# Attention and top-2 experts on one core: the product with the values in 64-row halves

## The reference

```python
x = L0_attn_x                                  # (8, 512, 128)
h = layernorm(x)
Q, K, V = (h @ W.T + b for each)               # 16 heads of 8
attn = softmax(Q @ K.T / sqrt(8), axis=-1)
x = x + (attn @ V) @ Wo.T + bo
h = layernorm(x)
logits = h @ Wr.T + br                         # 8 experts
top_v, top_i = top_k(logits, 2); top_w = softmax(top_v)
tgt2 = sum over the chosen e of top_w * (relu(h @ W1[e].T + b1[e]) @ W2[e].T + b2[e])
x = x + layernorm(h + tgt2) * gamma + beta
```

## Time and profile before

| what | value |
|---|---|
| median of 3 runs | 753.96 us (751.37 to 755.16) |
| the profiled execution | 752.29 us, its span 750.5 us |
| beats 0 to 127, first to last score pair A | 33.8 to 493.6 us |
| experts' stage | about 560 to 750.5 us |
| busy: TensorE, VectorE, ScalarE | 609.3, 489.0, 447.4 us |
| TensorE clock granted, mean | 0.91 |

### The profile page before, as it was taken

The page is one execution under the profiler, slowest core; times in us unless marked ns, Lnnn a source line. Parts: engine busy times, 40 slices in busy tenths (PEclk is TensorE's granted clock), DMA queues, the critical chain, the costliest instruction groups (busy, mean ns, idle before and its releaser), DMA issues. The chain is left out here.

```text
span 750.5 us, 13269 instructions
## 1 busy us (share of the span) xinstructions
PE 609.3 (81%) x3750; PEld 321.2 (43%) x3750; DVE 489.0 (65%) x1319; ACT 447.4 (60%) x945; POOL 242.6 (32%) x454
## 2 busy tenths in 40 slices
PE   2899999879988997987987998995229998999680
PEld 1633333323333432332332333332128988888530
DVE  3579989968967985985995887751204444444357
ACT  2718888867956965875885786683114444544333
POOL 5200101150240332214115005016425665555534
PEclk9959999989998998998998899899559999999976
DMA  7552122122122122022112211000121221221193
GB/s 219 195 153 66 44 69 83 49 67 74 37 85 72 33 84 84 26 65 89 49 47 70 65 45 48 6 0 30 50 83 54 65 66 56 69 66 57 47 238 98
DMA packets 54216, 54.47 MB, mean 73 GB/s; under 512 B 8286, under 2 KB 37514, under 8 KB 54164
## 3 DMA queue, kind: packets, MB, share of 16 engines
q1 hardware_dynamic: 48372, 44.19, 20.8%
q0 software_dynamic: 4416, 8.53, 3.2%
q10 hardware_dynamic: 1376, 1.13, 0.5%
HBM read 29.01 MB, written 24.81 MB: 72 GB/s over the span
## 5 line engine op out<-in xcount | busy, mean ns | idle before, releaser
L643 DVE TENSOR_REDUCE mneg<-s_psum 128x1 f32<-128x512 f32 x512 | 325.9, 684 | 89.5 <-PE s_psum L810 55.7
L546 ACT ACTIVATE pt<-st_psum 128x512 f32<-128x512 f32 x512 | 279.9, 598 | 93.3 <-PE st_psum L826 82.7
L826 PE MATMUL st_psum<-qs,ks 64*128 64x512 f32 x512 | 202.5, 471 | 24.8 <-ACT pt L546 19.4
L810 PE MATMUL s_psum<-ks,qs 64*128 64x512 f32 x512 | 208.3, 482 | 3.3 <-DVE mneg L643 2.1
L896 PE MATMUL pv_psum<-pt,vst 128*16 128x512 f32 x1024 | 142.8, 632 | 0.0
L810 PEld LDWEIGHTS s_psum<-ks,qs 64*128 64x128 f32 x512 | 84.4, 196 | 120.2 <-DVE mneg L643 94.9
L826 PEld LDWEIGHTS st_psum<-qs,ks 64*128 64x128 f32 x512 | 82.4, 193 | 69.1 <-ACT pt L546 52.7
L1099 ACT ACTIVATE hid<-h_psum,b1c 128x256 f32<-128x256 f32 x144 | 57.2, 474 | 71.2 <-PE h_psum L1204 69.3
L1062 POOL DMA_INDIRECT results<-res,goal_now x72 | 71.6, 994 | 33.7 <-issue 33.7
L1211 PE MATMUL y_psum<-w2t,hid 128*128 128x128 f32 x576 | 73.1, 280 | 0.0
L1211 PEld LDWEIGHTS y_psum<-w2t,hid 128*128 128x128 f32 x576 | 68.9, 194 | 0.9 <-issue 0.2
(11 more groups left out here) (164 smaller groups left out, 711.3 us busy)
## 6 DMA issues: line engine op xcount, KB each, us to landing
parts<-high SPq DMA_DIRECT2D x32, 256.0 KB, 3.0
ks<-parts SPq DMA_DIRECT2D x128, 48.0 KB
qs<-parts SPq DMA_DIRECT2D x128, 48.0 KB
lot<-sent SPq DMA_DIRECT2D x37, 132.0 KB
parts<-low SPq DMA_DIRECT2D x16, 256.0 KB, 3.1
got<-results SPq DMA_DIRECT2D x16, 256.0 KB, 5.1
xres<-in_L_attn_x_dram SPq DMA_DIRECT2D x8, 256.0 KB, 3.6
pt<-in_L_ffn_W_dram SPq DMA_DIRECT2D x1, 2048.0 KB, 14.5
```

The lines of the kernel that those rows point to most:

```text
L546: nc.scalar.activation(pt[:, n % PT_SLOTS, (g + 2) % 4, :], st_psum[:, k % ST_BANKS, :], ACT.Exp, scale=SCALE).then_inc(exp_done, 1)
L643: nc.vector.tensor_reduce(mneg[:, (n // 4) % 2, at:at + 1], s_psum[:, k % S_BANKS, :], AX_X, ALU.max, negate=True).then_inc(max_done, 1)
L810: mm(s_psum[:, k % S_BANKS, :], qs[rows, c, P * (n % 4):P * (n % 4) + P], ks[rows, c, g, :], start=True, stop=True).then_inc(s_made, 1)
L826: mm(st_psum[:, k % ST_BANKS, :], ks[rows, c, g, P * (n % 4):P * (n % 4) + P], qs[rows, c, :], start=True, stop=True).then_inc(st_made, 1)
```

## The change

The values product is split: each head's 128 rows become two halves of 64 rows, and each half has a bank of its own (`pv_psum` has 2 banks, and `st_psum` 2 instead of 3). The weights are windows of 32 columns in a new layout of `vst`, so that an even quad lands in rows 0 to 15 of each 32 and the odd quad after it in rows 16 to 31; one accumulation holds two quads, over 8 units. The heads of a quad are dealt out accordingly (`head_of`). The copy to `pvs` takes both banks once in 8 beats. TURN comes once in 8 beats (17 + 8m); for each of 4 pieces two matmuls with the identity add the halves. K moves from beat -13 to -11, so from 3 to 5 of 16. The transposes of W2 move from the beats -4 to -1 to the beats 1 to 4.

```diff
--- before.py
+++ after.py
@@ -56,7 +56,7 @@
 LAST_BEAT = GROUPS * (B - 1) + 38
 PLACE_STEPS = 1 + TILES + 5
 S_BANKS = 3
-ST_BANKS = 3
+ST_BANKS = 2
 PT_SLOTS = 4
 COMPLETE_LAG = 3
 KQ_LOADS = 2 * 4 + 1
@@ -75,13 +75,24 @@
     return q if r == 0 and 0 <= q < QUADS * B else None
 
 
+def per_pair(T, offset):
+
+    m, r = divmod(T - offset, 8)
+    return m if r == 0 and 0 <= m < QUADS * B // 2 else None
+
+
+def head_of(c, g):
+
+    return 8 * (c // 2) + 2 * g + c % 2
+
+
 def early_tasks(T):
 
     if (q := per_quad(T, 4)) is not None:
         yield "SHIFT", q
-    if (q := per_quad(T, 13)) is not None:
-        yield "TURN", q
-    for kind, offset in (("XT", -14), ("K", -13), ("Q", -10), ("V", 7), ("OT", 26), ("O", 27), ("X2T", 30),
+    if (m := per_pair(T, 17)) is not None:
+        yield "TURN", m
+    for kind, offset in (("XT", -14), ("K", -11), ("Q", -10), ("V", 7), ("OT", 26), ("O", 27), ("X2T", 30),
                          ("LOGITS", 31)):
         if (b := once(T, offset)) is not None:
             yield kind, b
@@ -118,7 +129,9 @@
 
 def expert_weights(T):
 
-    return range(2 * (T + 8), 2 * (T + 8) + 2) if -8 <= T < 0 else ()
+    if -8 <= T < -4:
+        return range(2 * (T + 8), 2 * (T + 8) + 2)
+    return range(E + 2 * (T - 1), E + 2 * (T - 1) + 2) if 1 <= T < 5 else ()
 
 
 def tiles(b, j=0, count=TILES):
@@ -180,11 +193,11 @@
 
         qs = sb("qs", [P, QUADS, S], F32R)
         ks = sb("ks", [P, QUADS, 4, S], F32R)
-        vst = sb("vst", [P, 2, TILES, H, 16])
+        vst = sb("vst", [P, 2, TILES, H // 2, 64])
         pt = sb("pt", [P, PT_SLOTS, 4, S])
-        pvs = sb("pvs", [P, S])
+        pvs = sb("pvs", [P, 2, S])
         onorm = sb("onorm", [P, TILES, D])
-        rden = sb("rden", [P, TILES, 4])
+        rden = sb("rden", [P, TILES, 8])
         mneg = sb("mneg", [P, 2, TILES * 4])
         shift_rows = sb("shift_rows", [TILES * 4, 2, P], F32R)
         xt, ot, xt2 = sb("xt", [P, 2, S]), sb("ot", [P, S]), sb("xt2", [P, S])
@@ -250,7 +263,7 @@
 
         s_psum = psum("s_psum", S_BANKS)
         st_psum = psum("st_psum", ST_BANKS)
-        pv_psum = psum("pv_psum")
+        pv_psum = psum("pv_psum", 2)
         side_psum = psum("side_psum")
 
         w_loaded, b_loaded, x0_loaded, x1_loaded, x_loaded = (
@@ -336,7 +349,7 @@
                 for g in range(4):
                     rows = slice(32 * g, 32 * g + 3 * HD)
                     dst = ks[rows, c, g] if w == 0 else qs[rows, c]
-                    sp.dma_start(dst.bitcast(F32), parts[b % 2, w, 4 * c + g]).then_inc(kq_in[c], 16)
+                    sp.dma_start(dst.bitcast(F32), parts[b % 2, w, head_of(c, g)]).then_inc(kq_in[c], 16)
 
             def beat(T):
                 if (q := per_quad(T, 4)) is not None:
@@ -345,7 +358,7 @@
                         sp.wait_ge(shift_in, 16 * q)
                     sp.dma_start(qs[SHIFT_ROW:P:32, q % QUADS].bitcast(F32), shift_rows[:, q % 2, :].bitcast(F32))\
                         .then_inc(shift_in, 16)
-                if (b := once(T, -13)) is not None:
+                if (b := once(T, -11)) is not None:
                     store_parts(0, b)
                 if (b := once(T, -10 if T < 0 else -8)) is not None:
                     store_parts(1, b)
@@ -397,7 +410,7 @@
             first_norm(0)
             nc.gpsimd.memset(vst[:], 0.0).then_inc(pool_consts, 1)
             pool.wait_ge(pool_consts, 4)
-            nc.gpsimd.memset(vst[:, :, :, :, HD:HD + 1], 1.0).then_inc(pool_consts, 1)
+            nc.gpsimd.memset(vst[:].rearrange("p z j h (a r) -> p (z j h a) r", r=32)[:, :, HD:HD + 1], 1.0).then_inc(pool_consts, 1)
             nc.gpsimd.memset(tail[:], 0.0).then_inc(tail_ready, 1)
             pool.wait_ge(tail_ready, 1)
             nc.gpsimd.memset(tail[:, :, D].bitcast(U32), NOWHERE).then_inc(tail_ready, 1)
@@ -522,8 +535,8 @@
                         act.wait_ge(pool_consts, 5)
                     if of >= 2:
                         act.wait_ge(pv_made, GROUPS * (of - 1))
-                    nc.scalar.copy(vst[:, of % 2, :, :, 0:HD],
-                                   side_psum[:, 0, :].rearrange("p (j h d) -> p j h d", j=TILES, d=HD))\
+                    nc.scalar.copy(vst[:, of % 2].rearrange("p j h (a r) -> p (j h a) r", r=32)[:, :, 0:HD],
+                                   side_psum[:, 0, :].rearrange("p (x d) -> p x d", d=HD))\
                         .then_inc(side_done, 1)
                 else:
                     dst = {"XT": xt[:, of % 2], "OT": ot[:], "X2T": xt2[:]}[kind]
@@ -531,11 +544,11 @@
 
             def beat(T):
 
-                if (q := per_quad(T, 12)) is not None:
-                    act.wait_ge(pv_made, 4 * q + 4)
-                    if q >= 1:
-                        act.wait_ge(side_made, SIDE["TURN", q - 1] + 1)
-                    nc.scalar.copy(pvs[:], pv_psum[:, 0, :]).then_inc(pv_copied, 1)
+                if (m := per_pair(T, 16)) is not None:
+                    act.wait_ge(pv_made, 8 * m + 8)
+                    if m >= 1:
+                        act.wait_ge(side_made, SIDE["TURN", m - 1] + 1)
+                    nc.scalar.copy(pvs[:], pv_psum[:]).then_inc(pv_copied, 1)
                 n = st_of(T)
                 for g in range(4):
                     if n is not None:
@@ -651,14 +664,14 @@
                                                    in1=high[:, w, :].bitcast(F32), op0=ALU.add, op1=ALU.subtract)\
                         .then_inc(side_done, 1)
                 elif kind == "TURN":
-                    c = of % QUADS
+                    at = 8 * (of % 2)
                     dve.wait_ge(side_made, SIDE["TURN", of] + 1)
-                    sums = side_psum[:, 0, :].rearrange("p (j g r) -> p j g r", j=TILES, g=4)
+                    sums = side_psum[:, 0, :].rearrange("p (j h r) -> p j h r", j=TILES, h=8)
                     nc.vector.reciprocal(rden[:], sums[:, :, :, HD]).then_inc(rden_done, 1)
                     dve.wait_ge(rden_done, of + 1)
                     nc.vector.tensor_tensor(
-                        onorm[:].rearrange("p j (h d) -> p j h d", d=HD)[:, :, 4 * c:4 * c + 4, :],
-                        sums[:, :, :, 0:HD], rden[:].unsqueeze(3).to_broadcast([P, TILES, 4, HD]),
+                        onorm[:].rearrange("p j (h d) -> p j h d", d=HD)[:, :, at:at + 8, :],
+                        sums[:, :, :, 0:HD], rden[:].unsqueeze(3).to_broadcast([P, TILES, 8, HD]),
                         ALU.mult).then_inc(side_done, 1)
                 elif kind == "O":
                     dve.wait_ge(side_made, SIDE["O", of] + 1)
@@ -849,7 +862,8 @@
                 elif kind == "TURN":
                     pe.wait_ge(pv_copied, of + 1)
                     for j in range(TILES):
-                        ins = nc.tensor.transpose(bank[:, P * j:P * j + P], pvs[:, P * j:P * j + P], ident[:])
+                        mm(bank[:, P * j:P * j + P], pvs[:, 0, P * j:P * j + P], ident[:], start=True, stop=False)
+                        ins = mm(bank[:, P * j:P * j + P], pvs[:, 1, P * j:P * j + P], ident[:], start=False, stop=True)
                 elif kind == "XT":
                     pe.wait_ge(xn_done, of + 1)
                     for j in range(TILES):
@@ -888,13 +902,17 @@
                 pe.wait_ge(exp_done, 4 * n + 4)
                 if n % GROUPS == 0:
                     pe.wait_ge(side_done, SIDE["V", b] + 1)
-                if n % 4 == 0 and q > 0:
-                    pe.wait_ge(pv_copied, q)
+                if n % 8 == 0 and n > 0:
+                    pe.wait_ge(pv_copied, n // 8)
                 if n == 0:
                     pe.wait_ge(pv_blank, 1)
                 for g in range(4):
-                    ins = mm(pv_psum[32 * g:32 * g + 16, 0, :], vst[:, b % 2, n % 4, 4 * (q % QUADS) + g, :],
-                             pt[:, n % PT_SLOTS, g, :], start=(n % 4 == 0), stop=(n % 4 == 3))
+                    at = 16 * (q % 2)
+                    for half in range(2):
+                        rows = slice(64 * half, 64 * half + 64)
+                        ins = mm(pv_psum[32 * g:32 * g + 32, half, :],
+                                 vst[rows, b % 2, n % 4, 4 * (q % QUADS // 2) + g, at:at + 32],
+                                 pt[rows, n % PT_SLOTS, g, :], start=(n % 8 == 0), stop=(n % 8 == 7))
                 ins.then_inc(pv_made, 1)
 
             def beat(T):
```

## The result

The change makes the kernel slower: 819.18 us, the median of four runs (815.68 to 819.90), against 752.78 us (751.37 to 755.16) for the kernel before. The ratio is 1.0881 with an interval of 1.0847 to 1.0915. The forecast was 770 us with a range up to 786: the direction is right, the size is not. The profiled execution took 819.55 us, its span is 817.7 us.

The account below looks back on a forecast made before the run. No engine is full in beats 0 to 127; the order of work inside a beat bounds the kernel. 5 + 10 + 14 - 2 + 4 - 11 - 1 = +19 us on 752.3 gave 771, forecast 770; range 735 to 786, from the bounds 757 to 788.

Parts of the forecast that it names:

- the stall: Unexplained standstill of 4.55 us in beat 56, alike in beats 40 to 120 by 16; could move a few us either way.
- Part 1: PV in 64-row halves: sixteen records beside each other, change of form still paid, 0.04 us a beat, +5 us.
- the first rival: Around PV: no change of form between 64-row products, saving 31 us, 740 us; sign PV to A under 0.9 us; chance 0.34.
- rival of halves in turn: PV's halves don't run beside each other, 0.85 us more in 122 beats, +104, 875 us; chance 0.04.
- Part 2: Two banks for turned scores: C and D wait for their own beat's exponentials, 1.3 us a round, +10 us, at most 37.
- the floor: Shortest beat with two banks, the next A at 3.05 us; side tasks of 0.9 us or more hide it.
- Part 3: TURN for two quads: sixteen records, 1.95 us, in beats 1 and 9, +14 us; VectorE's fewer operations -2 us.
- Part 4: Copy to `pvs` of 1024 columns takes 1.06 us, delaying exponentials in beats 0 and 8: +4 us.
- Part 5: K from beat 3 to 5, away from COUNTS: 2.1 us in each of 5 rounds, -11 us.
- Part 6: W2's transposes in beats 1 to 4: scores some 3 us earlier, 2 us taken back in the beats, -1 us.
- The parts cancel: Whole kernel: slack hides two banks' and the copy's costs, TURN costs 12 us; put at 752 us; chance 0.10.

Follow-up runs that it names:

- e9: The changed kernel unedited, on a chip without the stall: 761.98 us against 712.19 for the kernel before, 1.0698.
- e1: The kernel before with two banks instead of three for the turned scores, nothing else changed: 740.79 against 712.69 us, 1.0406.
- e13: The changed kernel with TURN transposing the first half's sums alone, the second half's copied but left out: 794.40 against 748.11 us, 1.0643.
- e3: The kernel before with two quads per PV bank over all 128 rows, three banks, TURN once in 8 beats: 710.16 us, 0.9970.
- e14: As e13, and the copy to `pvs` takes the first half's bank alone: 788.21 against 748.11 us, 1.0565.
- e4: As e3, with K in beat 5 instead of 3: 706.70 us, 0.9906 of the kernel before.
- e12: e4's kernel with an edit to spread GpSimd's indirect DMAs that did not take effect, in effect a repeat: 703.29 against 712.19 us, 0.9865.
- e2: The kernel before with W2's transposes moved to beats 1 to 4, nothing else changed: 716.42 against 712.69 us, 1.0052.
- e15: The changed kernel with one head of four in PV, weights of 32 columns, no reciprocal; one run on a chip with the stall: 790.23 us.
- e16: As e15, with PV's weights 128 columns wide, the score matmuls' own form; one run: 775.58 us.
- e7: As e3, with two banks for the turned scores: 780.72 us, 1.0415 of the kernel before.
- e10: The kernel before with an ineffective edit to spread indirect DMAs, in effect a repeat without the stall: 712.34 against 712.19 us, 0.9998.
- e5: The changed kernel unaltered, again on a chip with the stall: 813.38 against 748.48 us, 1.0895.
- e18: e4's kernel again, on a chip with the stall: 751.34 us, 0.9972 of the kernel before.
- e11: The changed kernel with an ineffective edit to spread indirect DMAs, in effect a repeat without the stall: 761.44 against 712.19 us, 1.0695.
- e8: The changed kernel with W2's transposes back in beats -4 to -1: 814.07 us, 1.0901 of the kernel before.
- e6: The kernel before unaltered, one run on a chip with the stall: 748.94 us.

## Why the prediction was off

Undisturbed by the stall the change costs 49.8 us (e9), where +19 was forecast. The parts measured one by one sum to 54.7; most were measured once, in one surrounding kernel, and each is uncertain by some us:

| part | forecast | measured | from |
|---|---|---|---|
| 1 PV in halves | +5 | +4 | a spacing, 0.03 to 0.04 us a beat; isolated by no run |
| 2 two banks | +10 | **+28** | e1; some 23 of it within the change |
| 3 TURN | +14 | +19 | e13 |
| 3 two quads, fewer operations | -2 | -2.5 | e3 |
| 4 copy | +4 | +6 | e14 |
| 5 K | -11 | -3.5 or -7.5 | e4 less e3, e12 less e3 |
| 6 W2 | -1 | +3.7 | e2 |
| stall | "a few us" | +17 | 66.4 less 49.8 |

The sum uses -3.5 for K. The 5 us that it has too many are within the scatter, but a cause of that size can be named: in e1 the scores begin 6.5 us late because the transposes of W1 and W2 both go through two banks. In the change W2's stand elsewhere, and the scores begin at 31.5 against 29.6 in e2 with three banks, 1.9 us late. So 4.6 of e1's 28 us are not in the change. The rows of parts 3 and 4 compare only in sum: the forecast counts each from the kernel before, e13 and e14 from a kernel with TURN and copy once in 8 beats, which e3 brings in. Together they were forecast at +16 and measured 22.5.

Two steps of the arithmetic were wrong by themselves. The sum of +19 belongs on the median of 753.96, which gives 773, not 770. And the range up to 788 "from the bounds" leaves room for +36 us, while the upper bounds of the parts add up to +96 (27 + 37 + 29 - 2 + 7 - 6 + 4); the +49.8 without the stall lies within those.

**Part 1 was right.** The change of form is not free, so the first rival (740 us) is refuted by its own criterion: PV to A is 1.02 us, not under 0.9, and e15 against e16 shows why. The cost of a change was taken as 0.09 and 0.20; it measured about 0.1 and 0.22. What the rival promised was too much, besides: taking 0.32 us out of each of 122 beats, 39 us, gave 14.7 in two single runs (e15 less e16), with the stall's 3.9 in it. Where the rest went is not shown. The eight tiles run beside each other: PV's sixteen records take 1.09 us against 1.05 for eight of 128 rows, which refutes the rival of halves in turn. In the beats without a side task of round 0 (9 to 11) a beat takes 3.15 to 3.16 us in e9 and 3.12 in e1, and PV to the next A is 1.02 us in place of 0.98, in the medians; 0.01 of that is there in e7 too, with windows of 32 columns over all rows. So the halves add about 0.03 to 0.04, 4 us.

**Part 2 is the step that failed most**: +28 us by itself and some 23 within the change, forecast +10. "D follows at about 1.75 ... the next A at 3.05" was right to 0.1 us. Median lengths of a beat, by its place in the round of 16, of e10 (before), e1 (two banks alone) and e9 (the whole change), none with the stall:

| beat of 16 | 0 | 1 | 2 | 3 | 4 | 5 | 8 | 9 | 10 | 12 | 13 | 14 |
|---|---|---|---|---|---|---|---|---|---|---|---|---|
| e10 | 2.76 | 3.51 | 3.01 | 4.85 | 4.66 | 2.90 | 2.69 | 2.90 | 2.98 | 3.26 | 2.89 | 3.84 |
| e1 | 3.18 | 3.81 | 3.14 | 4.88 | 3.27 | 3.12 | 3.18 | 3.11 | 3.12 | 3.18 | 3.11 | 3.71 |
| e9 | 3.68 | 4.33 | 3.61 | 3.73 | 3.30 | 3.40 | 3.73 | 4.33 | 3.22 | 3.26 | 3.15 | 3.68 |

With two banks no beat of these is under 3.11 us: the floor is there, as forecast, in the beats that were below it. A whole round grows by 1.96 us (from the means over seven rounds), against the forecast's 1.3. That mixes in the clock's dips in beat 4, five in e10 and two in e1: a round with K and without a dip takes 55.8 us in e1 and 53.2 in e2, 2.5 us more, so this half of the step was low by nearly a factor of two. Beats 0 and 8, where the copy holds the exponentials back, and beat 1 grew by 0.3 to 0.5 us, and so did beats 11 and 15 by 0.2 and 0.4, whose long tasks I had called cover. The larger half of the miss is the count: "some 122 beats that have scores and PV, 7.6 rounds" takes a bank's loss to be one of the steady beat. Beats 16 to 127 hold 13.3 of the 26.5 us between the two spans. The start holds 6.5 (the weights' transposes go through the same banks; I wrote +1 for it, under part 6, and within the change it is 1.9), beats 8 to 16 2.7, and the beats behind the last score pairs 5.7, for which I counted nothing. The upper bound of 37 us held.

**Part 3** had TURN's length right, and its place in the long beat. The block in beat 65, TensorE:

```profile
288.22 0.39 PE L823 MATMUL s_psum<-ks,qs 64*128 64x512 f32 x1
...
288.55 0.49 PE L865 MATMUL side_psum<-ident,pvs 128*128 128x128 f32 x2
...
290.21 0.39 PE L866 MATMUL side_psum<-ident,pvs 128*128 128x128 f32 x2
290.53 0.49 PE L839 MATMUL st_psum<-qs,ks 64*128 64x512 f32 x1
```

288.55 to 290.53 is 1.98 us, forecast 1.95. Beats 1 and 9 grew by 0.52 and 1.22 us from e1 to e9, forecast 0.86 and 1.2. Undoing it (e5 to e13) takes 0.52 and 1.18 us out of these two and 0.24 and 0.06 out of beats 2 and 10 behind them: 2.0 us a round, against the forecast's 2.06. The steady rounds were right, then; the rest of the 19 us lies in the stalled beat 8 and behind beat 127, and partly in the scatter of the medians. **Part 4**: the copy takes 1.01 us (forecast 1.06) and costs 6 us, not 4: the added 0.42 us comes through almost in full, 15 times.

**Part 5** was the "sure gain" of 11 us. The beats came out as forecast. The beats that answer to the earlier trace rows, the starts of A in beats 99, 100 and 101:

```profile
427.65 0.49 PE L823 MATMUL s_psum<-ks,qs 64*128 64x512 f32 x1
...
431.38 0.49 PE L823 MATMUL s_psum<-ks,qs 64*128 64x512 f32 x1
...
434.68 0.49 PE L823 MATMUL s_psum<-ks,qs 64*128 64x512 f32 x1
```

They take 7.03 us in place of 9.35, forecast about 7. But the reason was only half seen. Beats 100 and 116 of the kernel before, behind K with COUNTS and behind COUNTS alone (columns: stretch, its us, busy us of TensorE, its loads, VectorE, ScalarE and GpSimd, then TensorE's granted clock, DMA share and GB/s):

```profile
391.83:396.33 4.50, 3.82 (x18) 0.93 (x18) 2.71 (x5) 2.31 (x5) 2.26 (x10) 0.70 0.56 177
452.36:455.62 3.26, 2.58 (x18) 0.81 (x17) 2.49 (x5) 2.36 (x6) 1.35 (x7) 1.00 0.00 0
```

1.24 of the 2.37 us that the forecast read as COUNTS' wait and what it delays are beat 100 at the lower clock level, 4.50 us in place of 3.26. Where K stands apart from COUNTS (e4, e9), no such dip follows. K's gain in beats 16 to 127, 8.4 us from e3 to e4, is 1.7 a round in five rounds: 1.1 from the shorter beat 3 and 1.5 from the dip, which e3 has in all five, less 0.9 that K costs in beats 5 and 6, where the forecast took off 0.27. And K costs 1.0 and 1.4 us more in beats 0 to 8 and 8 to 16, where no COUNTS wait is saved. Up to the experts' stage e4 is 5.9 us and e12 6.2 us shorter than e3. Where the stall is, it grows by about what was gained (e18). **Part 6** had the earlier start right and the price in the beats wrong. The start after, TensorE:

```profile
31.50 1.22 PE L823 MATMUL s_psum<-ks,qs 64*128 64x512 f32 x3
34.73 3.18 PE L823 MATMUL s_psum<-ks,qs 64*128 64x512 f32 x5 [2.02 <-DVE mneg L656]
37.84 1.97 PE L947 MATMUL st_psum<-ident,pt 128*128 128x128 f32 x8
```

Eight records take 1.97 us here, where I took 1 us a beat. That is the length of the lower clock level, 1.2 GHz: in e2 they take 1.97 us as well, at 35.87 and 41.10, and the granted clock is 0.50 from 40 to 60 us. (The records of the trace after say 1.00 there; see the last section.) The kernel before passes through such a stretch too (0.57 from 40 to 60 us in e10), but its score matmuls are back under 0.6 us after 56.4 us, those of e2 after 67.6 and those of e9 after 70.4. So W2's transposes stand in the slowest beats of all and beats 0 to 8 take 10.7 us more, forecast 2 (e9; 8.9 in e11, where the short matmuls are back from 64 us on), for 2.0 us of earlier start. In the changed kernel undoing it also gives nothing (e8), since the transposes then go through two banks and the scores begin 6.6 us later.

**The parts cancel** (752) is refuted by e9: without the stall the parts add up to 50 us.

**The stall** accounts for the rest, 17 us; the prediction named it, left its cause open and allowed a few us for it. After, beats 7 and 8 take 13.6 to 14.9 us together, where e9 has 7.5 to 7.9: about 6.5 us a time, against 5.7 before. In the first pair of traces beats 16 to 127 hold only 2.0 of the 16.3 us by which the stall costs the change more (447.0 - 406.0 against 411.3 - 372.3), and 13.8 stand behind beat 127; with e5 and e6 it is 4.7 and 7.5. At the end a copy waits long after PV has run:

```profile
569.40 2.81 PE L913 MATMUL pv_psum<-pt,vst 64*32 64x512 f32 x48
...
577.14 0.96 POOL L503 DMA_INDIRECT sent<-xrow,placeu  x1 [0.30 <-issue]
579.65 1.01 ACT L551 COPY pvs<-pv_psum 128x1024 f32<-128x1024 f32 x1 [9.55 <-remote]
```

The last PV ends at about 572.2, and ScalarE's copy of its bank starts at 579.65, behind GpSimd's last indirect DMA. Where no stall is, the stretch from the last PV to the experts takes 43.0 us instead of 53.7. In the profiles that have it, the stall stands where the indirect DMAs run, and they run in the same beats where it is absent. Whether they are its cause, and why some chips have it, stays open: no run takes them away.

The version that beats both kernels is e4's: two quads per bank over all 128 rows, three banks for the turned scores, K in beat 5. It measured 0.991 and 0.987 where there is no stall and 0.997 (0.9946 to 0.9999) where there is.

## What to carry over

A bank taken from a ring between two engines is not priced by the steady beat alone: ask who else goes through the ring at the start and the end, and how much lateness it carried from one beat to the next; removing one of three cost 28 us here, and the steady beats were about half of it. Splitting a product into row halves gives nothing while its columns still differ from its neighbours': the array empties all the same. And a task moved out of a crowded beat pays what it costs in the rounds that were not crowded. When two beats are compared to price a move, compare the granted clock over both as well: half of the difference that priced K here was the clock's.

## What the runs showed of the hardware

- The same kernel takes 712 us on two chips and about 750 on three others and in the first comparison. Of the 40.0 us between the spans of before and e10, 39.0 lie in beats 16 to 127, 34 of them in beats 7 and 8 of six rounds. Behind each stalled beat 8 TensorE has a stretch at the lower clock level, 226.3 to 233.2 us for one (granted 0.50), so part of the price is the clock's. The mean granted clock over the span differs little, 0.910 and 0.924.
- A matmul's start in the trace can lie before its stream: in e16, A is recorded 0.46 us after PV, for 0.79 us, while PV still has a pass to run. B's start tells.
- The granted clock in a record and the length of the matmuls can differ: the trace of after grants 1.00 from 38 to 77 us, and there PV took 1.96 us at 71.11 and 1.09 us at 75.43. Lengths of one and the same matmul are the surer sign of the level.
- Behind the beat with K and COUNTS, in which TensorE is idle for 0.85 us (before 146.99 in e10), its granted clock can fall: it is 0.50 from 149.2 to 152.6 us there, and the beat takes 4.61 us in place of 3.26. That happens five, three and two times in the same five places of e10, e2 and e1, and nowhere in beats 16 to 127 of e4 and e9, where K stands apart.
- The Trainium skill (TensorE: Matmul & The Clock Gate, "The mechanism") says that weight loads overlap matmuls in flight only when the row group differs, though the same section also names a background weight buffer. Against the first, e16: PV's weights load at 202.91 in both row halves, while D's matmuls in both (202.81, 0.50 us) still run.
